# Two weight setups dissolved into the phases beside them, in a two-layer gated cross-attention kernel

## The reference, cut to what matters

```python
x = x + tanh(g_xattn[0]) * L0_xattn(layernorm(x), ctx, ctx, ...)    # tanh similarity attention, MLP 256-1024-256 (gelu)
x = x + tanh(g_ffn[0])   * L0_ffn(layernorm(x), weight, bias)       # fp8 quantised with ONE scale over all of x
x = x + tanh(g_xattn[1]) * L1_xattn(layernorm(x), ctx, ctx, mask)   # 16 heads of 16, masked softmax
x = x + tanh(g_ffn[1])   * L1_ffn(layernorm(x), ...)                # MLP 256-1024-256 (silu), int weights with scales
```

## Time and profile before

| | us |
|---|---|
| median of 3 runs | 1825.31 (1824.13 to 1828.05) |
| the profiled execution | 1827.43 |
| its span | 1825.3 |
| TensorE busy | 1627.5 (89%) |
| VectorE busy | 1377.1 (75%) |
| ScalarE busy | 1066.5 (58%) |
| GpSimd busy | 990.8 (54%) |

### The profile page before, as it was taken

How to read it: one execution, slowest core, us unless ns; L and a number is a source line. 1 busy time by engine, 2 the same in 40 slices (tenths; PEclk the granted TensorE clock), 3 DMA queues, 4 the chain that set the end, 5 groups by cost and what they waited for, 6 DMA issues and landing times.

```text
span 1825.3 us, 43348 instructions
## 1 busy us (share of the span) xinstructions
PE 1627.5 (89%) x14660; PEld 1282.4 (70%) x14660; DVE 1377.1 (75%) x3247; ACT 1066.5 (58%) x1950; POOL 990.8 (54%) x1811
## 2 busy tenths in 40 slices
PE   2899999999999991257999999999999999999997
PEld 2788888888888881134677777777777777777666
DVE  4577777777777754578888888888888888887642
ACT  3665666666666640135666666656565656666654
POOL 3456656656656430333465665656575747475535
PEclk9899999999999995578999999999999999999999
DMA  5221121121121003033232323222222322232200
GB/s 168 72 87 59 57 86 57 57 86 58 57 84 48 7 1 129 11 93 93 59 88 71 88 69 86 63 83 73 79 71 80 75 76 79 72 83 67 79 13 19
DMA packets 184316, 127.15 MB, mean 70 GB/s; under 512 B 15281, under 2 KB 183474, under 8 KB 183986
## 3 DMA queue, kind: packets, MB, share of 16 engines
q1 hardware_dynamic: 184242, 126.17, 24.0%
HBM read 100.94 MB, written 25.17 MB: 69 GB/s over the span
## 4 chain that ended last, share of the span: by engine, by line
PE 42%; ACT 7%; issue 5%; POOL 2%; SPq 1%; DVE 1%; DMA 1%; ACTq 0%; POOLq 0%
PE b_bank L1563 23%; PE b_bank L1632 6%; PE b_scoreT L1610 4%; PE b_scoreT L1614 3%; ACT L31 3%; ACT b_E L1222 2%; PE b_score L1594 2%; ACT b_Y L1292 2%; PE b_bank L1571 1%; PE b_bank L1713 1%; SPq L1077 1%; PE b_bank L1652 1%; SPq L1066 1%; DMA b_K<-k_dram 1%; POOL b_YT L1162 1%
## 5 line engine op out<-in xcount | busy, mean ns | idle before, releaser
L1222 ACT ACTIVATE b_E<-b_scoreT 128x1024 f32<-128x1024 f32 x256 | 263.2, 1028 | 211.2 <-PE b_scoreT L1614 210.9
L1402 DVE TENSOR_REDUCE b_nm<-b_score 128x4 bf16<-128x1024 f32 x256 | 313.2, 1223 | 46.3 <-PE b_score L1594 44.2
L1106 POOL TENSOR_TENSOR b_pool_fence<-b_pool_fence 128x1 f32<-128x1 f32 x288 | 61.9, 215 | 430.7 <-DVE b_mv L1361 322.0
L31 ACT ACT_TABLE_LOAD x156 | 200.1, 1283 | 64.7 <-PEq L788 52.1
L700 PE MATMUL bank<-W2T,G 128*128 128x256 f32 x1024 | 231.4, 379 | 0.0
L700 PEld LDWEIGHTS bank<-W2T,G 128*128 128x128 f32 x1024 | 191.9, 190 | 24.9
L368 POOL TENSOR_TENSOR pool_fence<-pool_fence 128x1 f32<-128x1 f32 x256 | 46.7, 194 | 277.2 <-DVE mv L536 145.9
L1563 PE MATMUL b_bank<-f,b_YT 128*128 128x256 bf16 x1536 | 190.0, 274 | 4.3 <-POOL b_YT L1162 4.3
L1563 PE MATMUL b_bank<-b_hT,f 128*128 128x256 bf16 x1536 | 186.3, 273 | 0.8 <-DVE b_res L1419 0.8
L667 PE MATMUL bank<-hT,W1T 128*128 128x256 bf16 x1536 | 178.3, 273 | 7.6 <-DVE hT L593 3.0
L667 PEld LDWEIGHTS bank<-hT,W1T 128*128 128x128 bf16 x1536 | 147.7, 98 | 36.2 <-ACT G L511 15.7
(11 more groups left out here) (215 smaller groups left out, 3605.4 us busy)
## 6 DMA issues: line engine op xcount, KB each, us to landing
b_Q<-q_dram SPq DMA_DIRECT2D x256, 64.0 KB, 2.6
b_K<-k_dram SPq DMA_DIRECT2D x256, 64.0 KB, 2.9
xin<-in_x SPq DMA_DIRECT2D x32, 256.0 KB, 4.3
X<-in_x SPq DMA_DIRECT2D x32, 256.0 KB, 4.4
ctxn<-in_ctx SPq DMA_DIRECT2D x32, 256.0 KB, 2.8
mask_in<-in_mask SPq DMA_DIRECT2D x32, 256.0 KB, 3.0
ctxt<-in_ctxT SPq DMA_DIRECT2D x32, 256.0 KB, 4.5
b_ctxt<-in_ctxT SPq DMA_DIRECT2D x32, 256.0 KB, 2.7
```

Of the source, the lines that this page charges most:

```text
L31: act.add_instruction(mybir.InstLoadActFuncSet(name=nc.get_next_instruction_name(), act_func_set_id=which, ins=[], outs=[]))
L1222: nc.scalar.activation(E[:, pair:pair + 2], scoreT_ps[:, :, :, :], ACT.Exp).then_inc(sig["E"], 1)
L1402: nc.vector.tensor_reduce(pair, score_ps[:, :, :, :], AX.X, ALU.max, negate=True).then_inc(sig["nm"], 1)
```

## The change

What it does, part by part:

- **First setup.** It is gone as a block. SyncE loads the small rows and WdT after the first batch's x, context and mask; W1, its columns and b1 after the second's; W2 after the third's. ScalarE makes the gate in iteration 0 and W1T's high part in iteration 1 ahead of the tanh; VectorE makes the low part and b1c at the end of iteration 2; TensorE the bias product in iteration 2, in a bank of the hidden layer. GpSimd makes the identities in iteration 0.
- **b2.** No ones and no b2r: GpSimd adds b2 (broadcast in b2_all) to f of each batch, after hn has been formed (`fb`), and f is added to the output as before.
- **Mask flag.** One reduction of the integer mask per batch (minimum of the absolute value); the comparison with 0 is done once, on 32 numbers, between the phases.
- **Second setup, attention and FFN weights.** They are loaded after the fifth iteration into W1's raw buffer, high parts at the ends of iterations 6 and 7 (ScalarE), low parts at the ends of 7 and 32 (VectorE), the output bias in iteration 7 (TensorE, then VectorE, with TensorE waiting for it), the FFN weight's all-reduce on GpSimd at the end of iteration 33, the small steps and wf on VectorE at the end of iteration 34.
- **Second setup, fc1 and fc2.** Loaded in the second phase's iterations 0 and 3 into the buffers Y and YT, which are free until the first hidden layer. VectorE dequantises at the ends of iterations 2 and 5, ScalarE makes the high parts there, VectorE the low parts at the ends of 3 and 5, and TensorE the bias product at the end of 2, in the bank of the transposed scores; the first transposed scores wait for b1f.
- **What is left between the phases** is the maximum of the normalised x and of the mask flags, one all-reduce and seven small steps.
- **V, nm and one_hot** are set by GpSimd at the end of the second phase's iteration 0.

The core of the diff (the removed setups and the moved loads, which the words above cover, are left out):

```diff
@@ phase_a, sync
+                if at_batch(b, 1):
+                    for dst, src in ((g_col[:, :], a["ln_g_col"]), (b_col[:, :], a["ln_b_col"]), (b1_raw[:, :], a["b1_col"]),
+                                     (raw_1[:, :, :], a["W1T"].rearrange("(c p) o -> p c o", p=P))):
+                        sp.dma_start(dst, src).then_inc(sig["W1_in"], 16)
...
+                if at_iteration(half, parity, 5):
+                    sp.wait_ge(sig["W1"], 1)
+                    for dst, src in second_loads:
+                        sp.dma_start(dst, src).then_inc(sig["second_in"], 16)
@@ phase_a, gpsimd
+                if m:
+                    pool.wait_ge(sig["hn"], done(m))
+                    for t in range(T):
+                        last = nc.gpsimd.tensor_tensor(f[m.parity][:, t, :], f[m.parity][:, t, :], b2_all[:, :], ALU.add)
+                    last.then_inc(sig["fb"], 1)
                 if u:
                     inverse_std(mvf, vef, rsf, "f", u)
+                if at_iteration(half, parity, NB + 1):
+                    pool.wait_ge(sig["peak_w"], 1)
+                    nc.gpsimd.partition_all_reduce(peaks_w[:, :], peak_w[:, :], P, MAX_OF_ALL).then_inc(sig["peaks_w"], 1)
@@ phase_a, scalar
+                if at_batch(b, 0):
+                    act.wait_ge(sig["W1_in"], 16 * 4)
+                    for c in range(C):
+                        last = nc.scalar.activation(W1T[:, 0, c], raw_1[:, c], ACT.Copy, scale=g_col[:, c:c + 1])
+                    last.then_inc(sig["W1hi"], 1)
...
+                for k in range(2):
+                    if at_iteration(half, parity, 6 + k):
+                        act.wait_ge(sig["second_in"], 16 * len(second_loads))
+                        for i in range(2 * k, 2 * k + 2):
+                            last = nc.scalar.activation(wqkvo[:, i, 0], raw_w[:, i], ACT.Copy,
+                                                        scale=DK ** -0.5 if i == 0 else 1.0)
+                        last.then_inc(sig["wqkvo_hi"], 1)
@@ phase_a, vector
-                    nc.vector.tensor_scalar(is_masked[:, :, :], mask_in[:, :, :], 0.0, None,
-                                            ALU.is_equal).then_inc(sig["is_masked"], 1)
-                    dve.wait_ge(sig["is_masked"], done(n))
-                    nc.vector.tensor_reduce(masked[:, bass.ds(n.number, 1)], is_masked[:, :, :], AX.XY,
-                                            ALU.max).then_inc(sig["masked"], 1)
+                    nc.vector.tensor_reduce(masked[:, bass.ds(n.number, 1)], mask_in[:, :, :], AX.XY, ALU.min,
+                                            apply_absolute_value=True).then_inc(sig["masked"], 1)
...
+                if at_batch(q, 0):
+                    dve.wait_ge(sig["W1hi"], 1)
+                    for c in range(C):
+                        last = nc.vector.scalar_tensor_tensor(W1T[:, 1, c], raw_1[:, c], g_col[:, c:c + 1], W1T[:, 0, c],
+                                                              ALU.mult, ALU.subtract)
+                    dve.wait_ge(sig["b1_mm"], 1)
+                    nc.vector.tensor_tensor(b1c[:, :], b1_raw[:, :], b1_ps, ALU.add).then_inc(sig["W1"], 1)
@@ phase_a, tensor
-                        nc.tensor.matmul(out_ps[:, t], G[w.parity][:, h, t * P:(t + 1) * P], W2T[:, h],
-                                         start=h == 0, stop=False)
-                    return nc.tensor.matmul(out_ps[:, t], ones3[:, 0:P], b2r[:, :], start=False, stop=True)
+                        last = nc.tensor.matmul(out_ps[:, t], G[w.parity][:, h, t * P:(t + 1) * P], W2T[:, h],
+                                                start=h == 0, stop=h == HC - 1)
+                    return last
...
+                if at_iteration(half, parity, 7):
+                    pe.wait_ge(sig["bv_rep"], 1)
+                    pe.wait_ge(sig["base"], done(q, back=1))
+                    for c in range(C):
+                        last = nc.tensor.matmul(U_ps[:, 0, :], bv_rep[:, c, :], raw_w[:, 3, c, :], start=c == 0,
+                                                stop=c == C - 1)
+                    last.then_inc(sig["bo_mm"], 1)
+                    pe.wait_ge(sig["gbo"], 1)
@@ phase_b, scalar
+                if at_iteration(half, parity, 5):
+                    act.wait_ge(sig["w2"], 1)
+                    nc.scalar.activation(f2[:, 0].rearrange("p h d -> p (h d)"), whole_YT, ACT.Copy).then_inc(sig["f2hi"], 1)
@@ phase_b, vector
+            def dequantised(loaded, step):
+                dve.wait_ge(sig[loaded], 32)
+                nc.vector.tensor_scalar(whole_Y, whole_Y.bitcast(I32), -128.0, None, ALU.add).then_inc(sig["less_" + step], 1)
+                dve.wait_ge(sig["less_" + step], 1)
+                nc.vector.tensor_tensor(whole_YT, whole_Y, whole_YT, ALU.mult).then_inc(sig[step], 1)
...
+                if at_iteration(half, parity, 2):
+                    dequantised("f1_in", "w1")
+                if at_iteration(half, parity, 3):
+                    dve.wait_ge(sig["f1hi"], 1)
+                    for c in range(C):
+                        last = nc.vector.scalar_tensor_tensor(f1[:, 1, c], whole_YT[:, c * HID:(c + 1) * HID],
+                                                              second["g_col"][:, c:c + 1], f1[:, 0, c], ALU.mult,
+                                                              ALU.subtract)
+                    last.then_inc(sig["f1lo"], 1)
+                    dve.wait_ge(sig["b1_mm"], 1)
+                    nc.vector.tensor_tensor(b1f[:, :], second["b1_raw"][:, :], b1_ps, ALU.add).then_inc(sig["b1f"], 1)
+                if at_iteration(half, parity, 5):
+                    dequantised("f2_in", "w2")
+                    dve.wait_ge(sig["f2hi"], 1)
+                    nc.vector.tensor_tensor(f2[:, 1].rearrange("p h d -> p (h d)"), whole_YT,
+                                            f2[:, 0].rearrange("p h d -> p (h d)"), ALU.subtract).then_inc(sig["f2lo"], 1)
@@ phase_b, tensor
+                def first_bias():
+                    pe.wait_ge(sig["w1"], 1)
+                    for k in range(HC):
+                        for c in range(C):
+                            last = nc.tensor.matmul(b1_ps[:, k:k + 1], whole_YT[:, c * HID + k * P:c * HID + (k + 1) * P],
+                                                    second["b_col"][:, c:c + 1], start=c == 0, stop=c == C - 1)
+                    last.then_inc(sig["b1_mm"], 1)
...
+                        pe.wait_ge(sig["b1f"], 1)
...
+                if at_iteration(half, parity, 2):
+                    first_bias()
```

More of the change, by code:

```diff
@@ L910, in setup_b @@
-    phase_b(nc, NB, out_d, ctxT_d, mask_d, X, mu1, rsq, scale_qk, gate, half_gate, ident, identb, minus_half,
-            wf, wqkvo, f1, f2, b1f, bq_col, bk_col, gbo_all, hfb_all, fb_all, any_masked)
-def phase_b(nc, NB, out_d, ctxT_d, mask_d, X, mu1, rsq, scale_qk, gate, half_gate, ident, identb, minus_half,
-            wf, wqkvo, f1, f2, b1f, bq_col, bk_col, gbo_all, hfb_all, fb_all, any_masked):
+            step(V_.tensor_tensor(scale_qk[:, :], back[:, :], second["back_w"][:, :], ALU.mult))
```

410 lines of the change are left out of this document (191 added, 219 removed).

## The result

| | before | after |
|---|---|---|
| median of 4 runs | 1824.78 us (1824.13 to 1828.05) | 1798.39 us (1795.39 to 1800.55) |
| ratio | | 0.9845, 95% interval 0.9828 to 0.9863 |
| the profiled execution, its span | 1827.43, 1825.3 | 1799.39, 1797.4 |
| TensorE, VectorE, ScalarE, GpSimd busy | 1627.5, 1377.1, 1066.5, 990.8 | 1618.2, 1354.6, 1074.4, 1041.7 |

A forecast was written before the change was run, and what follows sets the result against it. TensorE was taken to bound both phases' long stretches, with gaps of 23.1 and 50.8 us to dissolve. Terms -14.5 - 6.9 + 4.0 + 14.5 - 40.1 + 7.0 = -36.0 gave 1789 us, range 1770 to 1800.

The forecast's parts named there:

- start: First phase's start: loads move ahead, first tanh stands behind W1's load and high part; -14.5 us, from -17 to -10.
- ones: First phase, steady: 64 TensorE products of ones and b2r go, at 0.108 us each; -6.9 us.
- second weights in iterations 6 and 7: First phase: ScalarE's copies show 1.4 us, TensorE's wait for the output bias 2.5; together +4.0 us, bounds 1 and 6.
- end of the first phase: Iterations 33 and 34: GpSimd's configuration changes around the all-reduce +11.9, slower TensorE clock +2.6 us; bounds 0 and 18.
- seam: Between the phases: of 50.8 us, 10.7 remain, including 7.1 for GpSimd's configuration; -40.1 us, or -46.5 with a cheap configuration.
- second filling: Second phase's first iterations: earlier y gains, weight steps for fc1 and fc2 cost; altogether +7.0 us, bounds 0 and 19.
- rival 3: First phase: GpSimd's additions make it the bound and lengthen each batch; slower, 1863 us, chance 0.02.
- (1): Second phase's start: y comes 10.0 us after the start instead of 16.0, the inverse deviation earlier; -4.9 us.
- (2): Second phase, end of iteration 2: fc1's dequantising and bias product delay the scores; +4.0 us.
- (3): Second phase, end of iteration 3: fc1's low part on VectorE, transposed scores wait for b1f behind it; +2.4 us.
- Rival 1: GpSimd's configuration is no cost; the 7.1 us belong to two selects; -55.4 us, 1770 us, chance 0.17.
- Rival 2: Fillings hide nothing: second phase's steps all show, +19, and W1 lands at 19, +3.5; 1805 us, chance 0.15.

The follow-up runs named there:

- e3: Changed kernel with ScalarE making W1's high part behind the tanh of batch 0 instead of ahead of it: 1795.30 us, ratio 0.9819 to the kernel before.
- e6: Changed kernel with gate tanh, W1's high and low parts, bias product and W1/W2 loads moved later in the first phase's start: 1796.79 us, ratio 0.9836.
- e9: Changed kernel with the 64 products of ones back, ones and zero operand with 128 rows: 1805.33 us, ratio 0.9875 to the kernel before.
- e1: Changed kernel with the FFN weight's all-reduce merged into the one between the phases, wf steps moved to the second phase: 1785.49 us, ratio 0.9769.
- e4: Changed kernel with GpSimd's memsets of V, nm, one_hot and two selects in the second phase's iteration 1 instead of 0: 1797.05 us, ratio 0.9829.
- e5: Changed kernel with VectorE forming b1f ahead of fc1's low part instead of behind it: 1798.12 us, ratio 0.9845 to the kernel before.
- e2: As e1, with the maxima taken by TensorE transposes and VectorE, no all-reduce on GpSimd: 1775.33 us, ratio 0.9711 to the kernel before.
- e7: Changed kernel with the 64 products of ones back, with a 3-row operand of zeros: 1819.38 us, ratio 0.9962 to the kernel before.
- e8: Combination of e2, e6 and e5, with the sets in iteration 2 and fc1's bias products spread behind iteration 3's scores: 1767.00 us, ratio 0.9676.

## Why the prediction was right, and where its sizes were off

Differences of spans; the marks are those of the first table.

| step | forecast | measured |
|---|---|---|
| start | -14.5 | -12.0 (batch 2) |
| ones | -6.9 | -6.2 |
| second weights in iterations 6 and 7 | +4.0 | +3.8 |
| end of the first phase | +14.5 | +11.0 |
| seam | -40.1 | -41.0 |
| second filling | +7.0 | +15.0 |
| end | 0 | +1.5, of which 1.3 the last transfer |
| sum | -36.0 | -27.9 |

- **Start.** The mechanism was right (the tanh behind W1), the size 2.5 us off, still inside -17 to -10; the sign given for it, a first minimum near 34.5 us, failed (39.36, a lead of 9.6). The step that failed: "SyncE issues about 20 transfers at 0.5 us each" and "the queue is nearly empty behind it". Two of the issues took over 1.9, and W1 needed 7.3 us to land, not 5.5. Why 9.6 at the first minimum became 12.0 at the third is not shown. With the landing as forecast, the first minimum would still have been late by what stands next to that path (the context's landing at 21.7, the bias product, the next batch's x at 15.4 to 16.0), as e3 and e6 show; by how much, they leave open.
- **Ones.** 0.216 per batch was forecast, 0.215 measured against before and 0.222 in e9. Over the 27 intervals from batch 2 to 29 this is 5.8, and 0.4 behind. That the additions on GpSimd are free, shown by e9's period, was the forecast's own reason, and rival 3 (GpSimd as the bound) is out.
- **gbo and high parts.** From batch 2 to 29 the lead grows by 2.0, where the ones alone give 5.8: 3.8 lost, 3.5 of it between batches 4 and 5, as forecast.
- **End of the first phase.** The mechanism was the forecast one to the instruction. The two changes of configuration took 5.8 and 6.8 us where 7.1 stood for each, 1.6 in all, and the slow clock cost 1.7 instead of 2.6 (4.3 us between the starts of the hidden product and the next, 2.6 before); the other 1.0 of the 3.5 us is not accounted for. e1 takes the all-reduce away, and the eleven wf steps with it, and gets 11.3 back. That is less than the two gaps together (12.6), so nothing is left over for the steps; no run moved them alone. The Trainium skill's 5.95 us for freshly loaded code (GPSIMD Engine Reference, Instruction dispatch) is nearer than the 7.1 that I took to the two gaps ahead of an all-reduce (5.8 and 5.9); the one behind it, 6.8, is nearer to 7.1, and the last, 9.9, neither explains.
- **Seam.** 10.7 forecast, 9.9 measured, counted as in the forecast from the end of the last row maximum (689.12). The change of configuration took 5.9 instead of 7.1.
- **Second filling, the term that failed.** 15.0 instead of 7.0, inside the bounds of 0 to 19. Its parts, read from the marks: (1) "y is there 10.0 us after the start", -4.9: it was there after 12.6, since the gap for the configuration was 9.94 instead of 7.1, and what was left of the lead, 3.3 us at v(1), went in iteration 1, where the memsets and selects, costed at nothing behind the rounding, stretched VectorE's passes. Result +0.1; e4 gets 3.4 back in iteration 1, and loses 1.9 of it in the next. (2) The bias for fc1, +4.0: +6.7 at the first scores. Dequantising cost 4.6 at v(3), since it stands behind the last step of an iteration in which VectorE is the path, and not beside TensorE's wait; the product cost 2.1 more. (3) b1f, +2.4: +3.9, because the path is VectorE's f1lo (2.82) and the slower v behind it, not TensorE's wait (e5). (4) fc2, +5.5: +3.8. The sum of (1) to (4) with 0.5 of small shifts is the 15.0. Only (3) and the sets in (1) were tried by a run of their own. The scatter of this stretch between traces of nearly the same code, 4 us, is half the miss.
- **Rivals.** Rival 1 (the configuration costs nothing) is ruled out by e1 and e2. Rival 2 (the fillings hide nothing) had +19 for the second filling and a W1 landing at 19: both are nearer to the measured 15.0 and 20.9 than the forecast's 7.0 and 15.3, and so is its time, 1805, to 1798.39 than 1789.
- **Luck.** The second filling alone put the forecast 8 us off. That the result still lies in the range owes 3.5 us to the end of the first phase, which came cheaper than forecast for reasons of which 1.0 us is open; without them it would be near 1802.

Open: why the gap ahead of the second phase's first tensor_tensor is 9.94 us (9.4 to 10.2 in the eight traces that have it) where 7.1 stood before. Two things differ, and no run separated them. The first 1.5 us of it lie ahead of the end of VectorE's e (700.65), for which the tensor_tensor waits in any case; before, e had been ready for 2.3 us. And only this gap has DMA traffic beside it, with the loads for fc1 among it; the gaps around the all-reduces have a DMA share of 0.00, like the one before. The same windows as above, the changed kernel's gap first, then that of the kernel before:

```profile
699.10:709.00 9.90, 0.00 (x0) 0.00 (x0) 1.47 (x4) 3.69 (x3) 0.00 (x0) 0.50 0.65 238
749.60:756.67 7.07, 0.00 (x0) 0.00 (x0) 0.00 (x0) 0.00 (x0) 0.00 (x1) 0.50 0.00 0
```

## What to carry to other kernels

Price an all-reduce on GpSimd with both its changes of configuration, the one back to plain instructions too, wherever GpSimd's next result is waited for. A maximum of a few columns over 128 partitions is cheaper as two small transposes on TensorE with a reduction on VectorE between them (1.8 us here, against 5.8 + 0.4 + 6.8 or more). When work moves into an iteration, ask which engine is that iteration's path, and what GpSimd's instructions beside it do to VectorE's fast passes; a wait in the trace shows only where a delay ends up.

## What the runs showed of the hardware

- A product of 3 rows among products of 128: the next one starts 0.20 us after it instead of 0.11, the f32 group behind lasts 1.84 instead of 1.73, and each such product costs 0.38 us of the period instead of 0.11 (e7: 0.76 for two, e9: 0.22).
- GpSimd's configuration changes cost in either direction: 5.5 to 5.9 us ahead of an all-reduce, 6.7 to 7.5 behind the one in the first phase (seven traces), and 7.1 (before) or 9.4 to 10.2 (now, with DMA traffic beside it) ahead of the second phase's first tensor_tensor. In e2 and e8, which have no all-reduce, there is none of these gaps.
- A pass of 0.43 us on VectorE can take 4.25 beside GpSimd's addition and four memsets, longer than any single one of them (1.15 at most): in e4 it ends only behind the last.
- Two DMA issues on SyncE, 0.47 us as a rule, took 2.45 and 1.96 at 6.6 to 11.1 us, behind twelve others; the same two are slow in e3 (2.26, 2.21) and e6 (1.29, 2.27). The mean share of the DMA engines from 6 to 12 us was 0.59, so they were not all busy; what the issues waited for stays open.
